# The first expert layer's sums, computed with features on partitions and turned back to tokens

## The reference, cut to what matters

```python
gate_scores = softmax(einsum('bsd,ed->bse', x, Wg) + bg)       # 8 experts
topk_scores, topk_idx = top_k(gate_scores, 2)
expert_outputs = einsum('bsd,eod->bseo', x, W) + b             # every expert: 128x128
selected = take_along_axis(expert_outputs, topk_idx[..., None], axis=2)
output = sum(selected * topk_scores[..., None], axis=2)
x = layernorm(x + output)
```

## Time and profile before

| what | value |
|---|---|
| three runs | 1659.45, 1662.98, 1672.02 us; median 1662.98 |
| profiled execution, its own time | 1670.6 us |
| its span, first to last instruction | 1668.9 us |
| mean granted TensorE clock | 0.903 of full |
| busy over the span | PE 83%, PEld 37%, DVE 68%, ACT 51%, POOL 16% |
| PE passes by `w_exp` and `space` (128x128 float32) | 512, mean 325 ns |
| DVE multiplications of line 1842 (128x512) | 64, mean 684 ns |

### The profile page before, as it was taken

How to read it: one execution, slowest core, us unless ns; L and a number is a source line. 1 busy time by engine, 2 the same in 40 slices (tenths; PEclk the granted TensorE clock), 3 DMA queues, 4 the chain that set the end, 5 groups by cost and what they waited for, 6 DMA issues and landing times. The chain is left out here.

```text
span 1668.9 us, 20825 instructions
## 1 busy us (share of the span) xinstructions
PE 1386.6 (83%) x7344; PEld 618.1 (37%) x7344; DVE 1131.2 (68%) x2176; ACT 856.5 (51%) x1662; POOL 271.8 (16%) x336
## 2 busy tenths in 40 slices
PE   4678797888879877799999899999999999984570
PEld 2354573556446555122223322233222332222240
DVE  5647648565765555888887888878888788833115
ACT  5235215332441231277777677776777667772125
POOL 3221313213120301000000004000040000401361
PEclk9879997889897877599999999999999999996695
DMA  3070000110020255200111101111001100000224
GB/s 111 2 171 13 1 1 13 39 55 1 1 92 1 36 81 157 98 11 11 21 20 21 36 2 46 20 21 36 16 25 21 20 1 2 7 1 22 55 83 151
DMA packets 45965, 63.53 MB, mean 38 GB/s; under 512 B 8706, under 2 KB 33869, under 8 KB 44022
## 3 DMA queue, kind: packets, MB, share of 16 engines
q1 hardware_dynamic: 42790, 57.97, 14.3%
q0 software_dynamic: 3072, 4.23, 0.8%
HBM read 33.07 MB, written 31.15 MB: 38 GB/s over the span
## 5 line engine op out<-in xcount | busy, mean ns | idle before, releaser
L569 PE MATMUL ps<-space 128*32 128x512 f32 (+5 forms) x4608 | 867.2, 482 | 47.5 <-DVE smax L1988 16.5
L1988 DVE TENSOR_REDUCE smax<-ps 128x1 f32<-128x1024 f32 x512 | 605.3, 1220 | 126.1 <-PE ps L569 118.2
L1324 ACT ACTIVATE space<-ps 128x512 f32<-128x512 f32 x1024 | 556.5, 596 | 251.7 <-PE ps L569 250.3
L569 PEld LDWEIGHTS ps<-space 128*32 128x32 f32 (+5 forms) x4608 | 256.9, 111 | 632.5 <-ACT space L1324 320.9
L1422 POOL TENSOR_SCALAR eps_sum<-mv 128x4 f32<-128x4 f32 x32 | 7.3, 229 | 719.0 <-DVEq L1633 718.5
L1532 POOL DMA_INDIRECT expert_in<-space,slot x64 | 62.8, 982 | 267.0 <-DVE slot L2063 171.7
L569 PE MATMUL ps<-w_exp,space 128*128 128x128 f32 x512 | 86.8, 325 | 0.0
L1722 DVE SCALAR_TENSOR_TENSOR space<-space,conv_w 128x512 f32<-128x512 f32 x96 | 80.7, 850 | 4.1 <-ACT space L1150 1.6
L569 PEld LDWEIGHTS ps<-w_exp,space 128*128 128x128 f32 x512 | 74.5, 226 | 16.6 <-issue 16.6
L1197 ACT ACTIVATE btok<-ps 128x128 f32<-128x128 f32 x32 | 8.9, 277 | 138.7 <-DVE Gm L1740 69.5
L1842 DVE TENSOR_TENSOR space<-xnT,ps 128x512 f32<-128x512 f32 x64 | 42.1, 684 | 29.8 <-PE ps L569 29.8
(11 more groups left out here) (229 smaller groups left out, 1437.2 us busy)
## 6 DMA issues: line engine op xcount, KB each, us to landing
q_rows<-space SPq DMA_DIRECT2D x24, 256.0 KB, 2.5
k_rows<-space SPq DMA_DIRECT2D x24, 256.0 KB, 2.8
space<-k_rows SPq DMA_DIRECT2D x16, 384.0 KB, 5.1
space<-q_rows SPq DMA_DIRECT2D x16, 384.0 KB, 6.8
expert_out<-x_all SPq DMA_DIRECT2D x2, 2048.0 KB, 20.8
space<-expert_out SPq DMA_DIRECT2D x4, 1024.0 KB, 9.0
v_rows<-space SPq DMA_DIRECT2D x4, 668.0 KB, 3.6
space<-v_rows SPq DMA_DIRECT2D x4, 668.0 KB, 6.7
```

Of the source, the lines that this page charges most:

```text
L569: return nc.tensor.matmul(out, lhsT, rhs, start=first, stop=last)
L1324: nc.scalar.activation(prob[:, QUAD * (step % PROB_SETS) + unit % QUAD, :], bank(STB + unit % 2), ACT.Exp)\
L1988: v.tensor_reduce(smax[:, N % 2, i:i + 1], ps[:, b0:b0 + 2, :].rearrange("p k n -> p (k n)"), AX.X, ALU.max).then_inc(S.s_max, 1)
```

## The change

The sums are now gathered with output features on partitions. In a step the expert's matrix is the weights and 512 tokens of `xs` move: one float32 matmul for four. The bias is one matmul for four, `b_exp` as weights and `gT` moving. After a half's eight steps ACT copies bank 5 to `moeT` in SBUF (`evac_sums`), PE turns four tiles of it into bank 7 (`sums_back`), and DVE adds bank 7 to `x2`. Bank 7 is one of the two gate banks, so the gate rows of steps 10 and 11 both go to bank 6, and the gate rows of steps 11, 12 and 13 are issued later than before. One more step is done in turn c = 4. For H = 0 `sums_back` stands inside step 9 and DVE's addition after `expert_inputs(10)`; ACT's `evac_sums(p, 0)` stands in turn c = 5, ahead of `input_squares(m + 1)`. For H = 1 `evac_sums(p, 1)` stands after the loop, ahead of `mixed_squares(m, 0)`, and `sums_back(p, 1)` after `input_turned(m + 1)`.

```diff
-SUMS_AT = {4: (0, 1, 2), 5: (3, 4, 5, 6), 6: (7, 8, 9, 10), 7: (11, 12)}
+SUMS_AT = {4: (0, 1, 2, 3), 5: (4, 5, 6, 7), 6: (8, 9, 10), 7: (11, 12)}
+BACK_AT = E + 1
 SUMS_LAST = (13, 14, 15)
...
+        moeT = T[:, 3072:4096]
...
+        def gate_bank(k):
+
+            return 6 + (k + (k > BACK_AT + 1)) % 2
+
+        BACK_BANK = 7
...
                     if b + 1 < B:
                         pe.wait_ge(*((S.hid_ready, 2 * HID_TILES * (b + 2)), (S.skip_sum, 2 * (b + 2)))[H])
                     else:
-                        pe.wait_ge(S.xs_ready, 2 * E * (b + 1))
+                        pe.wait_ge(*((S.moe_added, 2 * (b + 1)), (S.xs_ready, 2 * E * (b + 1)))[H])
...
                     if b >= 1:
-                        pe.wait_ge(*((S.moe_added, 2 * b), (S.xs_ready, 2 * E * b))[H])
+                        pe.wait_ge(*((S.moe_sb, 2 * b), (S.xs_ready, 2 * E * b))[H])
                     transposes(lambda i: x1n[:, H * HT + i, :], bank(5 + H), S.xT_psum)

             def hidden(b, n):
...
+                if n == 0 and b >= 1:
+                    pe.wait_ge(S.moe_added, 2 * b)
...
                 elif k == 1:
                     pe.wait_ge(S.gT_sb, b + 1)
+                elif k == BACK_AT + 2:
+                    pe.wait_ge(S.xs_ready, 2 * E * b + k)
+                elif k == BACK_AT + 3:
+                    pe.wait_ge(S.moe_added, 2 * b + 1)
                 else:
                     pe.wait_ge(S.xs_ready, 2 * E * b + k - 1)
-                mm(bank(6 + k % 2), pick_rows[:, e, :], g3T[:, half(H)]).then_inc(S.gate_rows, 1)
+                mm(bank(gate_bank(k)), pick_rows[:, e, :], g3T[:, half(H)]).then_inc(S.gate_rows, 1)

             def expert_sum(b, k):
...
                     else:
-                        pe.wait_ge(S.moe_added, 2 * b + 1)
-                    for i in range(HT):
-                        mm(tile(bank(5), i), gT[:, (H * HT + i) * P:(H * HT + i + 1) * P], b_exp[:], i == 0, False)
+                        pe.wait_ge(S.moe_sb, 2 * b + 1)
+                    mm(bank(5), b_exp[:], gT[:, half(H)], True, False)
                 pe.wait_ge(S.xs_ready, 2 * E * b + k + 1)
-                if k + 2 < 2 * E:
+                if k == BACK_AT:
+                    sums_back(b, 0)
+                elif k == BACK_AT + 1:
+                    gate_rows(b, k + 1)
+                elif k == BACK_AT + 2:
+                    gate_rows(b, k + 1)
                     gate_rows(b, k + 2)
-                for i in range(HT):
-                    last = mm(tile(bank(5), i), tile(xs[:, k % XS_SLOTS], i), w_exp[:, e, :], False,
-                              e == E - 1 and i == HT - 1)
-                last.then_inc(S.xs_used, 1)
+                elif k + 2 < 2 * E:
+                    gate_rows(b, k + 2)
+                mm(bank(5), w_exp[:, e, :], xs[:, k % XS_SLOTS], False, e == E - 1).then_inc(S.xs_used, 1)
+
+            def sums_back(b, H):
+
+                pe.wait_ge(S.moe_sb, 2 * b + H + 1)
+                pe.wait_ge(S.xs_ready, 2 * E * b + (BACK_AT + 1 if H == 0 else 2 * E))
+                transposes(lambda i: tile(moeT, H * HT + i), bank(BACK_BANK), S.moe_turned)
...
                 if m is not None and m + 1 < B:
                     input_turned(m + 1)
+                if p is not None:
+                    sums_back(p, 1)
...
+            def evac_sums(b, H):
+                act.wait_ge(S.xs_used, 2 * E * b + E * (H + 1))
+                act.wait_ge(S.down_psum, 2 * b + 2)
+                if b >= 1:
+                    act.wait_ge(S.moe_turned, 2 * b)
+                nc.scalar.activation(moeT[:, half(H)], bank(5), ACT.Copy).then_inc(S.moe_sb, 1)
...
+                    if p is not None and c == HT + 1:
+                        evac_sums(p, 0)
                     if m is not None and m + 1 < B and c == HT + 1:
                         input_squares(m + 1)
                 if m is not None:
                     gated_squares(m, HT - 1)
+                if p is not None:
+                    evac_sums(p, 1)
+                if m is not None:
                     mixed_squares(m, 0)
...
             def expert_added(b, H):
-                dve.wait_ge(S.xs_used, 2 * E * b + E * (H + 1))
-                v.tensor_tensor(x2[:, own(H), :], x2[:, own(H), :], tiles4(5), ALU.add).then_inc(S.moe_added, 1)
+                dve.wait_ge(S.moe_turned, 2 * b + H + 1)
+                v.tensor_tensor(x2[:, own(H), :], x2[:, own(H), :], tiles4(BACK_BANK), ALU.add).then_inc(S.moe_added, 1)
...
                 expert_inputs(b, k)
-                if k == E + 1:
+                if k == BACK_AT + 1:
                     expert_added(b, 0)
```

More of the change, by code:

```diff
@@ L319, in build @@
             ln_var ln_rstd eps_added normed route_psum route_shift route_exp
-            gsel_ready g3_ready gT_psum gT_sb g3T_psum g3T_sb gate_rows xs_ready xs_used moe_added
+            gsel_ready g3_ready gT_psum gT_sb g3T_psum g3T_sb gate_rows xs_ready xs_used moe_sb moe_turned moe_added
             qk_psum v_psum q_ready k_ready q_part k_part q_rest k_rest v_ready rows_stored v_stored dve_step
@@ L1841, in expert_inputs @@
                     dve.wait_ge(S.xs_used, 2 * E * b + k + 1 - XS_SLOTS)
-                v.tensor_tensor(xs[:, k % XS_SLOTS], xnT[:, half(H)], bank(6 + k % 2), ALU.mult).then_inc(S.xs_ready, 1)
+                v.tensor_tensor(xs[:, k % XS_SLOTS], xnT[:, half(H)], bank(gate_bank(k)), ALU.mult).then_inc(S.xs_ready, 1)
             def expert_added(b, H):
-                dve.wait_ge(S.xs_used, 2 * E * b + E * (H + 1))
-                v.tensor_tensor(x2[:, own(H), :], x2[:, own(H), :], tiles4(5), ALU.add).then_inc(S.moe_added, 1)
+                dve.wait_ge(S.moe_turned, 2 * b + H + 1)
+                v.tensor_tensor(x2[:, own(H), :], x2[:, own(H), :], tiles4(BACK_BANK), ALU.add).then_inc(S.moe_added, 1)
                 dve.wait_ge(S.moe_added, 2 * b + H + 1)
```

## The result

| | median | lowest to highest | runs |
|---|---|---|---|
| before | 1667.45 us | 1659.45 to 1672.02 | 4 |
| changed | 1685.03 us | 1682.14 to 1689.19 | 4 |

The ratio is 1.0116 with a 95% interval of [1.0087, 1.0144]: 19.3 us by the ratio, 14.5 to 24 by its interval, and 17.6 between the two medians. The median of before is of four runs here, 4.5 us above that of the three which the forecast of 1680 started from. The profiled execution of the changed kernel took 1682.1 us, the fastest of its four; the one of before took 1670.6, above its median.

A forecast was written before the change was run, and what follows sets the result against it. PE was taken as the engine that never rests inside the sums. The terms summed to +16.7 us on the profiled 1670.6, giving 1687; lowered by 7.6 to the runs' median, the forecast was 1680 us, range 1671 to 1691.

The forecast's parts named there:

- Passes: Expert sums on PE: two passes of 512 columns for eight of 128 save 0 to 8 us; taken as -2 us.
- rival of loads on the path: Sums: if a load costs what a pass costs, fewer loads give 52 us, 1628 us; chance 0.05.
- Squares behind the evacuation: Slots 1 and 2: ACT's late squares delay POOL and PE's chunk 6; +5.7 us each, +11.4 us.
- Absorbed: Rival: ACT or POOL reach the late squares in another order, 11.4 and 5 fall away, 1663 us; chance 0.12.
- Clock: Two terms: PE at 1.2 GHz behind the new waits, +5 us; low clock behind half 0's addition going away, -4.2 us.
- The sums hold the high clock: Rival: 512-column passes get or keep the high clock in the sums, up to 22.7 us back, 1661 us; chance 0.13.
- well below 35: Sign that the forecast is wrong: PE's half-clock time in the sums falls well below 35 us.
- Half 0: Slots 1 to 3: PE's waits around DVE's addition go, turned tiles come; -0.5 us a slot, -1.5 us.
- inputs 11 to 13: Slots 1 to 3: gate rows issued late make input 12 come one input later; 0.6 us a slot, +1.8 us.
- half 1's tail: Slots 1 to 4: copy, turning and drain after the last pass, 1.3 us each, not hidden; +5.2 us.
- slot 4: Half 0 there: no chunk work covers the copy, turning costs 0.72, input 11 comes later; +1.0 us.

The follow-up runs named there:

- passes_alone: Kernel before with only the new matmul form for steps and biases, copy and turning left out (sums added the wrong way round); 1665.04 us, ratio 0.9986.
- squares_first: Changed kernel with ACT doing the next input's squares ahead of the copy of half 0's sums; 1666.85 us, ratio 0.9988 to the kernel before.
- before_late_squares: Kernel before with ACT's squares of the next input made to wait until step 6 of the sums is done; 1680.05 us, ratio 1.0076.
- root_later: Changed kernel with POOL's root of the next input's norm moved behind chunk 6's decays; 1662.61 us, ratio 0.9956 to the kernel before.
- two_banks: Kernel before with half 1's sums in bank 7, its gate rows one step ahead in bank 6, half 0 added one input later; 1702.53 us, ratio 0.9964.
- two_banks_root_later: Kernel before with half 1's sums in bank 7 and POOL's root behind chunk 6's decays; 1694.01 us, ratio 0.9925.
- root_later_again: Changed kernel with POOL's root behind chunk 6's decays, run again on the other chip; 1701.11 us, ratio 0.9973 to the kernel before.

## Why the prediction was right, and where it was not

- **Passes: right.** The step fell by 0.04 us, and passes_alone shows nothing more in it. By the estimate from the section "Back-to-back issue gap" of the Trainium skill's "TensorE: Matmul & The Clock Gate" it would have fallen by 0.39; the traces of both kernels disagree for float32 (1.41 and 1.37 us). The rival of loads on the path is refuted.
- **Squares behind the evacuation: right, and it decides.** 5.74 and 5.73 us against a forecast of 6.0 with today's 0.27 in it; none in slot 3. squares_first and before_late_squares show it from both sides, and with it gone the change costs nothing that was measured. "Absorbed" is refuted. Taking the wait out gave 21 us (17 to 26 if squares_first's ratio is held), where the forecast has 16.4 for wait and clock together; putting it in cost 12.7 (8 to 17). In the traces the attention starts 15.2 us earlier without it (666.5 for 681.7), of which PE's waits for POOL are 11.1, and 9.2 later with it.
- **Clock: right where it was looked for, wrong in the sum.** Behind the two waits 4.7 us were lost for the 5 forecast, and no stretch at the low clock begins behind half 0 in slot 3. But in the traces 9.4 us came back elsewhere, not 4.2, in slots 2 to 4: the two terms together were +0.8 and measured -4.7. That is nearly the whole gap between +16.7 and the +10.8 of the ledger. Nor does the clock behind the waits show as a net cost: without them (squares_first) PE's busy time at the low clock was 20.3 us for 30.1 in slot 1, but 37.4 for 29.7 in slot 2, and 106.4 for 106.8 in the four slots. How much of it belongs to the change is open: the same kernel, root_later, had 116.9 us in its trace on one chip and 101.9 on the other, and the thirteen traces lie between 85.3 and 116.9.
- **"The sums hold the high clock": not borne out.** Between the first and the last expert pass of the four sequences PE was busy at the low clock for 44.7 us before (6.8, 10.2, 16.3 and 11.4) and for 39.7 after (19.9, 9.4, 6.8 and 3.6), 9.5 of them behind the new waits. So the sign "well below 35" wasn't there, and steps at 2.54 us still were. Where the waits behind the late squares are gone as well, it is 26 to 30 us (four traces of three kernels). But two_banks and two_banks_root_later, with the old passes and no wait ahead of half 1, have 17.7 and 15.5, and passes_alone, with the new passes and that wait, 35.0. One trace each, and the whole slots don't follow as clearly, but the order speaks for PE's wait ahead of half 1 and not for the form of the passes.
- **Half 0, inputs 11 to 13, half 1's tail, slot 4: right in the trace**, each within 0.6 us of its term. The tail's share of the time was tried twice and is not settled.
- **The total: right in part by luck.** The forecast was +16.7 us, and the times gave 17.6 by the medians and 19.3 by the ratio. Yet the terms measured in the traces sum to +10.8, with a clock term of the other sign. The traces show one execution each, that of before slower than its median and that of after the fastest of its four, and the six or so microseconds that the medians differ by beyond them are in no term. The stated range, 1671 to 1691, is also narrower than the ends given with the terms, which add up to some 1667 to 1699; 1685 lies in either.
- **Missed:** the same wait in slot 0. It costs before and after alike, so the forecast did not suffer, but reading slot 0 would have shown beforehand what that wait costs when nothing covers it.

## What to carry to other kernels

When a new wait is put into an engine's stream, list what stands behind it on that engine, and follow that to the engine that runs out of work. Here the wait cost more than the work that was saved: two independent function calls in the right order, or the root behind the decays, gave back the 1.2%, while the new form of the passes alone earned some 2.3 us, not told from nothing. And when a chain is hidden by some work in most rounds, look at the round that lacks this work: its price stands there already.

## What the runs showed that I had not expected

The same program takes 1669.9 us on one chip and 1709.2 or 1706.6 on another. The slots nearly agree (660.0 and 664.1 us to the attention for root_later on the two chips); the difference lies between there and the end, 995 to 999 us in the traces of before, after and the first four kernels and 1036 to 1047 in the seven of the other chip, with the same attention. root_later_again has seven stretches at the low clock that begin there, 149 us in all, where the same kernel had three, 102 us, on the first chip. Three of the extra ones begin at 1013, 1225 and 1447 us, behind a time in which PE stood idle and for which the profile names no engine, or ACT, which stood idle itself. ACT and DVE have 28.7 and 22.3 us of waits there that the profile puts down to no instruction it has (it calls them `remote`), and none in root_later's trace. POOL's gathers ran on at their usual pace meanwhile. Two of the extra stretches, each with the idle time ahead of it (columns as above):

```profile
1005.00:1013.00 8.00, 3.23 (x16) 1.00 0.17 56
1013.00:1027.00 14.00, 11.77 (x35) 0.51 0.05 17
1218.00:1225.00 7.00, 4.90 (x29) 0.98 0.14 40
1225.00:1245.00 20.00, 15.00 (x45) 0.50 0.07 20
```

What stops the three engines there was not tried.
